# Value stage of an attention and filter kernel in another order: first sums in a place of their own, norms and softmax two groups later, function tables and low-rank mixing sooner

## The reference, cut to what matters

```
h   = einsum over channels of x with a 32x32 matrix chosen per batch      # mixing
q, k, v = h @ Wq + bq, h @ Wk + bk, h @ Wv + bv                           # 512 -> 4096, 32 heads
q, k = rms_norm over all 4096 (gq, gk)                                    # var + 1e-6
x   = x + softmax(q k^T / sqrt(128)) v @ Wo + bo
K   = 2 Re sum_n Ct[h,n] exp(dtA[h,n] * l),  l = 0..511                   # 32 filters from exp, sin, cos
y   = (causal convolution of x's channels with K + D x) * length mask
x   = x + y @ ffn_w + ffn_b + low-rank terms: sum over 16 loras of gate[b,n] * A_n, then B_n, and a shared pair
```

## Time and profile before

| | |
|---|---|
| median of 3 runs | 848.13 us (846.91 to 849.87) |
| the profiled execution: its own time, its span | 848.47 us, 846.4 us |
| PE busy | 811.2 us (96% of the span) |
| DVE busy | 640.1 us (76%) |
| POOL busy | 515.8 us (61%) |
| ACT busy | 327.5 us (39%) |
| mean granted TensorE clock | 0.986 |

### The profile page before, as it was taken

One profiled execution on the slowest core, in us unless ns is written; L12 is line 12 of the kernel. 1 busy time (PEld: TensorE's weight loads), 2 busy tenths in 40 slices (PEclk: granted clock), 3 DMA queues, 4 the chain that ended last, 5 costly groups with the idle time before them and its releaser, 6 DMA issues.

```text
span 846.4 us, 15196 instructions
## 1 busy us (share of the span) xinstructions
PE 811.2 (96%) x6089; PEld 663.8 (78%) x6089; DVE 640.1 (76%) x652; ACT 327.5 (39%) x371; POOL 515.8 (61%) x449
## 2 busy tenths in 40 slices
PE   8899999999999999987999999799999999997988
PEld 7587888888888888866887888688888888884466
DVE  5989998888888888879974957897788897423341
ACT  4555555555555555651322130531432324042310
POOL 5888993333333333098999951571499999991140
PEclk9999999999999999998999999999999999999989
DMA  5131111111111114004442522304923823216601
GB/s 169 50 79 52 50 50 50 50 50 50 50 50 50 50 50 149 0 2 149 174 168 106 199 100 100 113 1 149 203 98 128 320 100 112 87 50 220 142 26 75
DMA packets 80687, 81.80 MB, mean 97 GB/s; under 512 B 26012, under 2 KB 61180, under 8 KB 78604
## 3 DMA queue, kind: packets, MB, share of 16 engines
q1 hardware_dynamic: 79856, 81.16, 29.6%
q10 hardware_dynamic: 796, 0.15, 0.1%
HBM read 64.90 MB, written 16.40 MB: 96 GB/s over the span
## 4 chain that ended last, share of the span: by engine, by line
PE 54%; POOL 26%; DVE 7%; issue 6%; DMA 3%; SPq 3%; ACT 1%; POOLq 0%; DVEq 0%
PE psum L816 11%; PE psum L817 10%; PE psum L818 10%; POOL gated L719 8%; POOL a_sum L722 5%; POOL b_sum L722 5%; PE psum L763 3%; PE psum L764 3%; PE psum L765 3%; PE psum L851 2%; SPq L438 2%; PE psum L1000 1%; POOL prod L636 1%; POOL ang L637 1%; DMA la_nat<-in_lora_a 1%
## 5 line engine op out<-in xcount | busy, mean ns | idle before, releaser
L486 POOL TENSOR_TENSOR w_raw<-w_raw 128x256 f32<-128x256 f32 x32 | 45.2, 1413 | 136.6 <-DMA w_raw<-in_wk 136.0
L816 PE MATMUL psum<-t_hi,w_hi 128*128 128x512 f32 x256 | 104.0, 406 | 2.4 <-DVE qk_sb L1527 1.1
L818 PE MATMUL psum<-t_hi,w_lo 128*128 128x512 f32 x256 | 99.8, 390 | 0.0
L817 PE MATMUL psum<-t_lo,w_hi 128*128 128x512 f32 x256 | 99.8, 390 | 0.0
L1280 ACT ACTIVATE sq<-qk_sb 128x1024 f32<-128x1024 f32 x31 | 32.9, 1063 | 143.2 <-issue 139.2
L1535 DVE TENSOR_TENSOR sumsq<-sumsq,sq 128x1024 f32<-128x1024 f32 x62 | 80.4, 1298 | 0.0
L816 PE MATMUL psum<-mix_hi,w_hi 128*128 128x512 f32 x192 | 75.1, 391 | 2.3 <-DVE w_lo L1452 1.2
L818 PE MATMUL psum<-mix_hi,w_lo 128*128 128x512 f32 x192 | 74.8, 390 | 0.0
L817 PE MATMUL psum<-mix_lo,w_hi 128*128 128x512 f32 x192 | 74.8, 390 | 0.0
L1319 ACT ACTIVATE at_hi<-psum,params 128x512 fp32r<-128x512 f32 x64 | 43.9, 687 | 74.2 <-PE psum L1000 74.1
L1000 PE MATMUL psum<-p_blocks,v_sb 128*128 128x128 f32 x512 | 60.5, 280 | 4.9 <-DVE at_lo L1720 4.9
(11 more groups left out here) (272 smaller groups left out, 2116.9 us busy)
## 6 DMA issues: line engine op xcount, KB each, us to landing
v_sb<-v_scr_dram SPq DMA_DIRECT2D x6, 2048.0 KB, 8.0
v_scr_dram<-v_sb SPq DMA_DIRECT2D x9, 1024.0 KB, 4.2
w_raw<-in_wq SPq DMA_DIRECT2D x32, 256.0 KB, 2.9
w_raw<-in_wk SPq DMA_DIRECT2D x32, 256.0 KB, 3.2
wv_raw<-in_wv SPq DMA_DIRECT2D x16, 512.0 KB, 4.6
toep<-kpad_dram SPq DMA_DIRECT2D x2, 4096.0 KB, 15.1
wo_raw_a<-in_wo SPq DMA_DIRECT2D x4, 1024.0 KB, 5.2
wo_raw_b<-in_wo SPq DMA_DIRECT2D x4, 1024.0 KB, 5.5
```

The costliest lines, as they stand in the source:

```text
L816: mm(bank(n), wh, hi[:, c, tok], start=(i == 0), stop=False)
L817: mm(bank(n), wh, lo[:, c, tok], start=False, stop=False)
L818: last = mm(bank(n), wl, hi[:, c, tok], start=False, stop=(i == 1))
```

## The change: what it does

- **First sums.** For t = 0 the sum k1 + k2 goes to a new tile `first_s1`, and q1 - k1 goes over k1, so neither waits for DVE's split of q1. `value_raw` reads j = 3 and j = 5 from there. SP loads the next k1 two splits later. POOL starts its iotas only after `wvlo_ok` 4, since `first_s1` lies under `expo`.
- **Norms.** DVE does `norms()` before `split_value(2)`. `inverse_norms` moves from i = 1 to 9, `soft_max(0)` from 3 to 11, `soft_norm(0)` from 5 to 13, `spread(0)` from 25 to 24. ACT's first exponential moves from i = 4 to 12.
- **Angles.** The products that make `ang` and `expo` are cut into the pieces of `reduce_angles` and a new `exponents`. `value_sums(3)` runs before the last angles. `tables` runs at i = 24 of the value stage instead of in unit 0.
- **Unit 0.** `split_o(0, 0)` runs before group 27's additions. `soft_max(1)` runs after `attn_out(0)`.
- **bo.** The adds of bo to `acc` move behind POOL's chain of small operations that ends in `tab_ok`; `acc` is loaded in two halves, bo before them.
- **Filters and low-rank mixing.** PE makes the filters at unit 1, not 2. SP issues the eight loads of the low-rank matrices before unit 2's values.

```diff
+            if t == 0 and j == 3:
+                return flat2(first_s1[:])
+            if t == 0 and j == 5:
+                return flat2(wv_raw[:, R_K1])
...
             for t in range(3):
-                sp.wait_ge(wvlo_ok, 7 * t + 4)
-                load_v(t + 1, R_K1)
+                if t > 0:
+                    sp.wait_ge(wvlo_ok, 7 * t + 4)
+                    load_v(t + 1, R_K1)
...
                 load_v(t + 1, R_Q1)
+                if t == 0:
+                    load_v(1, R_K1)
...
-            sp.wait_ge(vp_mm, 2 * 28)
-            sp.dma_start(acc[:], x_rows).then_inc(acc_in, 16)
             sp.wait_ge(ang_ok, 1)
             sp.dma_start(bo_rows, every_partition(bo, FEAT)).then_inc(bo_in, 16)
+            sp.wait_ge(vp_mm, 2 * 28)
+            for half in (1, 0):
+                sp.dma_start(acc[:, HG * half:HG * half + HG, :], x_rows[:, HG * half:HG * half + HG, :]).then_inc(acc_in[half], 16)
...
-            load_unit(2)
-            next_weights(1)
             sp.wait_ge(kern_mm, 1)
             for c in range(KC):
                 sp.dma_start(la_nat[quadrant(c)], ...
             for c in range(KC):
                 sp.dma_start(lb_nat[:, c], ...
-            load_unit(3)
+            load_unit(2)
             sp.wait_ge(kern_d, 4)
             for q in range(4):
                 sp.dma_start(kpad[8 * q:8 * q + 8, 0:FEAT]...
+            next_weights(1)
+            load_unit(3)
...
+            def first_sums():
+                gp.tensor_tensor(s1, k1, k2, ALU.add).then_inc(vs_ok, 1)
+                gp.tensor_tensor(k1, q1, k1, ALU.subtract).then_inc(vs_ok, 1)
+                pool.wait_ge(p4_mm, HEADS - 1)
+                pool.wait_ge(wlo_ok, HEADS)
+                gp.tensor_tensor(s2, k2, k1, ALU.subtract).then_inc(vs_ok, 1)
+                pool.wait_ge(wvlo_ok, 2)
+                gp.tensor_tensor(q2, q2, s2, ALU.subtract).then_inc(vs_ok, 1)
...
-            value_sums(0)
+            first_sums()
             pool.wait_ge(vq_mm, 1)
+            pool.wait_ge(wvlo_ok, 4)
...
             reduce_angles(0, 16)
             value_sums(1)
+            exponents(0, 16)
             reduce_angles(16, 32)
+            value_sums(2)
+            exponents(16, 32)
             reduce_angles(32, 48)
-            value_sums(2)
-            reduce_angles(48, 64)
-            reduce_angles(64, 67)
+            reduce_angles(48, 56)
+            value_sums(3)
+            reduce_angles(56, 67)
+            exponents(32, 48)
             gp.memset(sm("t2"), 0.0).then_inc(ang_ok, 1)
-            value_sums(3)
...
-            pool.wait_ge(bo_in, 16)
-            pool.wait_ge(acc_in, 16)
-            for g in (4, 5, 6, 7, 0, 1, 2, 3):
-                gp.tensor_tensor(acc[:, g, :], acc[:, g, :], bo_rows, ALU.add).then_inc(acc_set, 1)
...
             gp.tensor_tensor(u_tab[:], ang[:, 32:48, :], ang[:, 48:64, :], ALU.add).then_inc(tab_ok, 1)
+            pool.wait_ge(bo_in, 16)
+            for half in (1, 0):
+                pool.wait_ge(acc_in[half], 16)
+                for g in range(HG * half, HG * half + HG):
+                    gp.tensor_tensor(acc[:, g, :], acc[:, g, :], bo_rows, ALU.add).then_inc(acc_set, 1)
...
             for n in range(7):
-                if n == 2:
+                if n == 1:
                     pe.wait_ge(tab_ok, 1)
...
+            norms()
             split_value(2)
-            norms()
             split_value(3)
...
-                if i == 1:
-                    inverse_norms()
+                if i == 27:
+                    split_o(0, 0)
                 if j > 0:
                     for pair in range(2):
                         value_post(t, j, pair)
-                if i == 3:
+                if i == 9:
+                    inverse_norms()
+                if i == 11:
                     soft_max(0)
-                if i == 5:
+                if i == 13:
                     soft_norm(0)
-                if i == 25:
+                if i == 24:
                     spread(0)
-            soft_max(1)
...
             for n in range(8):
                 attn_out(n)
+                if n == 0:
+                    soft_max(1)
```

More of the change, by code:

```diff
@@ L587, in _ @@
                     combine(i * 2 + j, j, i * 32 + 32)
+            def first_sums():
+                q1, q2, k1, k2 = (flat2(wv_raw[:, n]) for n in range(4))
+                s1, s2 = flat2(first_s1[:]), value_raw(2, 0)
+                pool.wait_ge(wv_in[R_K1], 16)
+                pool.wait_ge(wv_in[R_K2], 16)
+                gp.tensor_tensor(s1, k1, k2, ALU.add).then_inc(vs_ok, 1)
+                pool.wait_ge(vs_ok, 1)
+                pool.wait_ge(wv_in[R_Q1], 16)
+                gp.tensor_tensor(k1, q1, k1, ALU.subtract).then_inc(vs_ok, 1)
+                pool.wait_ge(vs_ok, 2)
+                pool.wait_ge(p4_mm, HEADS - 1)
+                pool.wait_ge(wlo_ok, HEADS)
+                gp.tensor_tensor(s2, k2, k1, ALU.subtract).then_inc(vs_ok, 1)
+                pool.wait_ge(vs_ok, 3)
+                pool.wait_ge(wvlo_ok, 2)
+                gp.tensor_tensor(q2, q2, s2, ALU.subtract).then_inc(vs_ok, 1)
             def value_sums(t):
@@ L622, in _, with exponents @@
             step(gp.tensor_scalar(quarter_pi[:], quarter[:], 2 * PI, None, ALU.mult))
-            step(gp.tensor_tensor(ang[:], repeat(mult[:], 2, 32), repeat(sm("th"), 1, 67), ALU.mult))
-            step(gp.tensor_tensor(expo[:], repeat(mult[:, 0:48], 2, 32), repeat(sm("xr"), 1, 48), ALU.mult))
+            def exponents(a, b):
+                ex = expo[:, a:b, :]
+                step(gp.tensor_tensor(ex, repeat(mult[:, a:b], 2, 32), repeat(sm("xr"), 1, b - a), ALU.mult))
+                step(gp.tensor_scalar(ex, ex, 88.0, -87.0, ALU.min, ALU.max))
             def reduce_angles(a, b):
@@ L630, in reduce_angles @@
                 pr = prod[:, 0:b - a, :]
+                step(gp.tensor_tensor(an, repeat(mult[:, a:b], 2, 32), repeat(sm("th"), 1, b - a), ALU.mult))
                 step(gp.tensor_scalar(k, an, 1.0 / (2 * PI), None, ALU.mult))
@@ L996, in attend @@
                         pe.wait_ge(alo_ok, OCT * n + (u - 3))
-                    if n == 2 and u == 2:
+                    if n == 1 and u == 2:
                         pe.wait_ge(kern_ok, 1)
@@ L1242, in split_value @@
                 t, j = jj // 7, jj % 7
-                if j == 2 or j >= 3 and j < 6:
-                    act.wait_ge(vs_ok, 4 * t + (0, 0, 3, 2, 4, 1)[j])
+                if 2 <= j < 6:
+                    order = (0, 0, 3, 1, 4, 2) if t == 0 else (0, 0, 3, 2, 4, 1)
+                    act.wait_ge(vs_ok, 4 * t + order[j])
                 else:
@@ L1328, in split_o, with tables @@
                               ACT.Copy).then_inc(wohi_ok, 1)
+            def tables():
+                act.wait_ge(ang_ok, 1)
+                sc.activation(sm("thx"), sm("xr"), ACT.Tanh, scale=0.5).then_inc(fn_ok, 1)
+                sc.activation(ang[:], ang[:], ACT.Sin).then_inc(fn_ok, 1)
+                sc.activation(expo[:], expo[:], ACT.Exp).then_inc(fn_ok, 1)
             split_value(2)
@@ L1349, in _ @@
                     first_out(t, 1)
-                if i == 4:
+                if i == 12:
                     exp_scores(0)
+                if i == 24:
+                    tables()
             split_o(0, 0)
-            def tables():
-                act.wait_ge(ang_ok, 1)
-                sc.activation(sm("thx"), sm("xr"), ACT.Tanh, scale=0.5).then_inc(fn_ok, 1)
-                sc.activation(ang[:], ang[:], ACT.Sin).then_inc(fn_ok, 1)
-                sc.activation(expo[:], expo[:], ACT.Exp).then_inc(fn_ok, 1)
             for n in range(8):
-                if n == 2:
+                if n == 1:
                     act.wait_ge(kern_mm, 1)
@@ L1373, in _ @@
                     exp_scores(1)
-                    tables()
                 if n + 2 < 8:
@@ L1690, in spread, with split_o @@
                 last.then_inc(p_ok, 1)
+            def split_o(m, part):
+                hi, lo, raw = ((wo_hi_a, wo_lo_a, wo_raw_a), (wo_hi_b, wo_lo_b, wo_raw_b))[part]
+                dve.wait_ge(wohi_ok, 2 * m + part + 1)
+                v.tensor_tensor(lo[:].rearrange("p h n -> p (h n)"), raw[:].rearrange("p h n -> p (h n)"),
+                                hi[:].rearrange("p h n -> p (h n)").bitcast(F32), ALU.subtract).then_inc(wolo_ok, 1)
+            norms()
             split_value(2)
-            norms()
             split_value(3)
@@ L1721, in attn_out @@
                                            at_hi[:, u, :].bitcast(F32), ALU.add, ALU.subtract).then_inc(alo_ok, 1)
-            def split_o(m, part):
-                hi, lo, raw = ((wo_hi_a, wo_lo_a, wo_raw_a), (wo_hi_b, wo_lo_b, wo_raw_b))[part]
-                dve.wait_ge(wohi_ok, 2 * m + part + 1)
-                v.tensor_tensor(lo[:].rearrange("p h n -> p (h n)"), raw[:].rearrange("p h n -> p (h n)"),
```

(1 more changed line is left out.)

17 lines of the change are left out of this document (6 added, 11 removed).

## The result

The changed kernel takes **823.54 us** (median of 6 runs, 823.27 to 824.36). The kernel before took 848.25 us (median of 6, 846.38 to 849.87) beside it. The ratio is 0.9713 (95% interval 0.97 to 0.9727). Forecast were 817.0 with a range to 825, so the direction and the range hold, and the gain is 24.7 us where 31.1 were worked out. The profiled execution took 823.41 us, its span is 821.2, the mean granted clock 0.996 (before: 0.986).

The account below looks back on a forecast made before the run. PE was taken to bound the kernel, with time to win only in its gaps and the half clock after them. The terms summed to 31.1 us off the profiled 848.47, hence 817.0 us, range 813 to 825.

Parts of the forecast that it names:

- Start of the value stage: Up to group 4: earlier first sums and norms leave PE no gap, 11.9 us gained, bounds 8 and 12.4.
- Rest of the value stage: Group 4 to unit 0: POOL's sums arrive in time although PE comes 12 us sooner, 1.2 us gained.
- The credit of 1.2 for group 16: Value stage: POOL's second sums end 11 us before group 16, so PE's gap there of 1.2 us goes.
- Unit 0: Unit 0's attention: DVE reaches its first at_lo by 518, PE wants it at 519, 6.7 us gained.
- Unit 1: DVE's work in unit 0, which POOL's adds can stretch, holds PE at unit 1's first at_lo: 0.8 us lost, 0 to 3.
- Tail: Unit 7's projection to the end: earlier mixing and transfers, fewer waits and more clock, 12.1 us gained.
- rival 1: Tail: transfers stay late, b_all taking over 3.5 us longer; price up to 4.3 us, 821 us; chance 0.10.
- The low-rank product: Tail: the product that took 5.31 us at clock 0.69 gains 0.8 us, 0 to 1.6.
- Rival 2: Groups 9 or 23: POOL is late, its steps stretched beside DVE; price 2 to 6 us, 819 to 823; chance 0.09.
- Rival 3: Value stage, unit 0 and tail: half clock comes without gaps, 8.5 us of credits lost, 825.5 us; chance 0.12.
- Rival 4: Start of value stage: another wait takes over from the first sums, 8 us of 11.9 lost, 825 us; chance 0.06.
- Rival 5: Unit 2 waits because load_unit(2) sits behind the small-row loads; 864 us at five times the issue time; chance 0.02.

Follow-up runs that it names:

- experiment 7: The kernel before with only the first sums in their place and DVE's norms ahead of the split of group 2: 845.30 us, ratio 0.9963.
- experiment 8: The changed kernel with the inverse norms back at group 1 of the value stage instead of group 9: 823.82 us, ratio 0.971.
- experiment 1: The changed kernel with soft_max(0) at i = 17, its exponential at 18 and soft_norm(0) at 20, instead of 11, 12, 13: 825.42 us, ratio 0.9728.
- experiment 3: The changed kernel with POOL's value_sums(2) waiting for the end of soft_max(0)'s third operation on DVE: 827.79 us, ratio 0.9758.
- experiment 4: The changed kernel with POOL's exponents(16, 32) ahead of value_sums(2) instead of behind it: 819.70 us, ratio 0.967.
- experiment 5: The changed kernel with POOL adding bo on one column per group instead of 512, so most of the addition is left out: 819.53 us, ratio 0.9669.
- experiment 10: The changed kernel with exponents first, softmax at 17 and 20, spread(0) at 25, and unit 2's exponential and soft_norm(2) in unit 1: 822.17 us, ratio 0.9691.
- experiment 11: The changed kernel with only unit 2's exponential and soft_norm(2) postponed to unit 1, behind its attention output: 823.28 us, ratio 0.9698.
- experiment 12: The changed kernel with exponents(16, 32) ahead of value_sums(2), and unit 2's exponential and soft_norm(2) postponed to unit 1: 821.65 us, ratio 0.9683.
- experiment 6: The changed kernel with the filters made at unit 2 and SP's loads in the order of before: 839.93 us, ratio 0.9902.
- 9: The changed kernel with exponents(16, 32) ahead of value_sums(2), softmax at 17, 18 and 20, and spread(0) at 25: 819.54 us, ratio 0.9654.
- experiment 2: The changed kernel with the inverse norms at group 6 instead of 9: 823.07 us, ratio 0.9702.

## Why the prediction was right, and where it was short

The time came out in the range and most terms by their mechanism. Two terms, in the rest of the value stage and in unit 1, went the wrong way or far beyond their size for one common reason, DVE stretched by POOL.

**Start of the value stage: right in size (12.8 for 11.9, bounds 8 and 12.4), partly for another reason.** POOL's first sums and the norms did what was forecast: `inv_norm` took 0.42 us (3.98 before), and the norms together 0.95 us (366.81 to 367.76) where I took 1.1. (Inverse norms and softmax move by eight groups, from 1, 3 and 5 to 9, 11 and 13, and not by two as the title says.) The prediction gave the cuts of POOL's products 1.5 us of cost and nothing else. Experiments 7 and 8 put the larger part there: with the first sums alone 5.0 us are gained, with the rest of the change but the inverse norms left in place 12.3, and what differs at the gap is the 5.63 against 1.10 us of the two multiplications.

**Rest of the value stage: the term that failed.** The prediction says that inverse norms and softmax "overrun DVE's share of groups 9 and 11 by 2 to 3 us, but additions are wanted two groups later". That priced DVE's operations at 1.22 us each although POOL's sums lie beside them. They were stretched by 3.2 us, and PE waited 2.25 us and then had half the clock for part of group 14: 4.0 us lost, shown by experiments 1 and 3. The same paragraph put POOL's `ang_ok` at "496 to 500"; it was 502.8. POOL waited 3.06 us for DVE's split of group 14 and 1.23 for the one of group 15, and its budget had no waits at all; experiment 4 fills the first and gains 2.1 us up to unit 0's projection. The credit of 1.2 for group 16 was right.

**Unit 0: 5.2 for 6.7.** "blocks zeroed at about 503", first `at_lo` "by 518": they were 506.3 and 522.7. It is POOL's lateness again, and not DVE's amount of work, since experiment 4 takes the gap away.

**Unit 1: 4.2 lost where 0.8 was forecast, with 3 as the bound.** The mechanism (POOL's adds stretch DVE) was named, and its price was too low: 2.8 us of stretching, plus the clock after the gap. From DVE's first `at_lo` of unit 0 to the first of unit 1 it took 32.7 us (522.70 to 555.38) where 31.4 were worked out, and 29.9 in experiment 5. PE wanted it 1.82 us sooner, so the 32.7 of cover were in fact about 30.9. Of the 4.2 us, the gap at a clock of 1.00 accounts for 2.4, as experiment 4 shows (9.51 us of attention against 7.06 in later units). The rest is the 0.18 and half the clock, which followed the same gap in some runs and not in others. The gap needs both POOL's adds and DVE's amount of work: experiment 5 removes it by the one, experiments 10 to 12 by the other, but these bring it back a unit later.

**Tail: 13.9 for 12.1.** `toep`, `b_all` and the transposes came as forecast, and rival 1 (late transfers) is out. The low-rank product gained 1.6 us of clock instead of 0.8 (3.71 us for 5.31). Experiment 6 puts the gain on the earlier filters and mixing; the loads ahead of `load_unit(2)` cost nothing that can be seen, since unit 2 has no gap in the changed kernel.

**Rivals.** Rival 2 (POOL late beside DVE) is the nearest to what happened: POOL was late, at `p_blocks`, and at group 14 the parts were exchanged, since PE was held there not by POOL's sums but by DVE, stretched by POOL. Rival 3 (half the clock without a gap) did not come. In every stretch read here with a clock below 1.00 a gap of PE lies just ahead. Rivals 4 and 5 did not come either.

The stage's end is held by three things that take turns: DVE's additions at group 14, POOL's chain up to `p_blocks`, and DVE's arrears into unit 1. That is why 4 us gained in one (1, 9) are mostly given back at the next. What remains open is whether POOL's adds of bo can lie where DVE has only PSUM or one-operand work; no run tried it with the whole addition. The best complete kernel here is experiment 4's, with 9 as fast; 1.8 us of its gain hang on the clock in unit 1.

## What to carry to other kernels

- When a step is moved, price it by what the *neighbouring* engine does at the new place. An operation of VectorE with two SBUF operands beside an operation of GpSimd with two costs up to the length of GpSimd's. Here, once GpSimd's long operations were cut into pieces, moving VectorE's away from them gained nothing more.
- An engine's budget is work plus waits. A chain that lies between two of another engine's steps is not started sooner by less work ahead of it; fill the wait with work that has no such condition.
- Before you move work to a later place to close a gap, ask whether the engine has slack there. Here the gap went along.
- Before you credit an edit with a gain, find the gain in the marks. Half of experiment 4's lay behind a gap that the edit had not touched.

## What the runs showed of the hardware

**DVE and POOL exclude each other rather than share.** DVE's 128x256 multiplications took 0.68 and 0.42 us in experiment 8, and 2.74 and 2.89 beside POOL's 3.81 and 2.84 in experiment 7, each ending 0.3 us after POOL's. In the changed kernel the two engines took turns around group 14: POOL's 3.37 us ended 2.25 us behind the end of DVE's 2.05 us (434.16), and DVE's 3.41 us ended 1.08 us behind POOL's (436.41). That is in each case near the operation's own time alone, 2.40 and 1.22. The Trainium skill says in SBUF — State Buffer, section Who interferes with whom, that a VectorE operation with two SBUF inputs and a GpSimd operation that reads SBUF take a shared pair of ports exclusively, and the second waits for the whole of the first. The runs agree for POOL's two-operand operations, and DVE's reductions and additions from PSUM, which have at most one input in SBUF, stayed at 1.22 beside them. In experiment 8, though, DVE's multiplications of 0.68 and 0.42 us ran from 373.74 to 374.87 inside a one-operand operation of POOL, here the rows of POOL:

```profile
373.53 1.50 POOL L660 TENSOR_SCALAR turns<-ang 128x512 f32<-128x512 f32 x1
375.11 1.05 POOL L661 TENSOR_TENSOR turns<-turns,quarter 128x512 f32<-128x512 f32 x1
```

So a one-operand operation of POOL did not hold DVE up to its end, where the rule makes no such exception; the 0.68 is at most 0.26 us of delay. The other way round such operations were delayed: in the changed kernel POOL's one-operand 128x512 operation at 451.74, beside DVE's two-operand splits, took 2.35 us instead of the 1.50 shown above.

**A gap's length does not tell the clock.** After 2.25 us of idle PE before group 14 the granted clock was 0.67. In experiment 8 it was 1.00 after 1.76 us at the same place, and 1.00 after 2.18 us before group 27. The gap of 1.82 us in unit 1, with the same 32 matmuls behind it, was followed by 0.68 in the changed kernel and in experiments 2 and 8, and by 1.00 in experiments 1, 3 and 4. In unit 2 the 3.08 us of experiment 11 were followed by 1.00 and the 2.76 us of experiment 10 by 0.50. What decides it no run here shows. The stretches of experiment 8:

```profile
439.90:445.00 5.10, 5.06 (x22) 4.22 (x23) 5.10 (x5) 0.00 (x0) 4.76 (x6) 1.00 0.64 263
513.10:518.70 5.60, 5.58 (x24) 4.42 (x24) 5.60 (x6) 0.00 (x0) 4.31 (x17) 1.00 0.54 201
```
